# Values of all tokens and keys of the second block by seven products instead of eight

## What is computed

```python
x = x + tanh(g_xattn[0]) * xattn(layernorm(x), ctx, ctx, Wq, Wk, Wv, Wd)
x = x + tanh(g_ffn[0])   * ffn(layernorm(x), gate, up, down)
# xattn: Q = q @ Wq.T  (32 heads of 128)
#        K = k @ Wk.T, V = v @ Wv.T  (8 heads of 128)
#        softmax(causal(Q K^T / sqrt(128))) V, then @ Wd.T; sequences of 64 tokens
# ffn:   w_eff = w * (su @ sv) for gate, up and down; silu(gate) * up, then down
```

## Time and profile before

| | |
|---|---|
| median of three runs | 1504.87 us (1504.06 to 1505.11) |
| the profiled execution | 1504.84 us, its span 1503.0 us |
| PE busy | 1486.7 us, 99% of the span, 7,586 matmuls |
| DVE / POOL / ACT busy | 1081.2 (72%) / 730.1 (49%) / 603.6 us (40%) |
| keys and values | until 193.8 us |
| queries (32 quads) | from 193.8 to about 523 us |
| granted PE clock | 2.4 GHz level, mean 0.999 |
| DMA | 214.4 MB, mean 143 GB/s |

### The profile page before, as it was taken

One profiled execution on the slowest core, in us unless ns is written; L12 is line 12 of the kernel. 1 busy time (PEld: TensorE's weight loads), 2 busy tenths in 40 slices (PEclk: granted clock), 3 DMA queues, 4 the chain that ended last, 5 costly groups with the idle time before them and its releaser, 6 DMA issues.

```text
span 1503.0 us, 21016 instructions
## 1 busy us (share of the span) xinstructions
PE 1486.7 (99%) x7586; PEld 1197.8 (80%) x7586; DVE 1081.2 (72%) x1630; ACT 603.6 (40%) x1040; POOL 730.1 (49%) x636
## 2 busy tenths in 40 slices
PE   8999999999999999999999999999999999999998
PEld 7898978778888777777777777777788888888886
...
GB/s 182 184 195 223 180 195 267 250 239 259 351 304 258 196 184 112 115 132 113 123 145 118 119 127 113 113 153 82 21 44 57 49 56 50 113 50 56 50 57 70
DMA packets 114806, 214.37 MB, mean 143 GB/s; under 512 B 9616, under 2 KB 47760, under 8 KB 112656
## 3 DMA queue, kind: packets, MB, share of 16 engines
...
...
## 4 chain that ended last, share of the span: by engine, by line
PE 91%; DVE 5%; issue 1%; DMA 1%; POOL 1%; ACT 0%; SPq 0%; DVEq 0%; ACTq 0%; POOLq 0%
PE bank L450 67%; PE bank L612 4%; PE bank L574 4%; PE bank L726 3%; PE bank L725 3%; PE bank L727 3%; PE bank L583 2%; PE bank L597 2%; DVE x_st L1057 1%; PE bank L508 1%; DVE er L1078 1%; DMA c_raw<-in_ctx_t 1%; DVE el L1078 1%; DVE X L1243 1%; PE bank L636 0%
## 5 line engine op out<-in xcount | busy, mean ns | idle before, releaser
L1389 POOL TENSOR_TENSOR wd_lo<-wd_raw,wd_hi 128x512 fp32r<-128x512 f32 x64 | 91.4, 1448 | 368.7 <-ACT wd_hi L844 368.7
L450 PE MATMUL bank<-wd_hi,o_hi 128*128 128x512 f32 x512 | 205.7, 402 | 0.0
L450 PE MATMUL bank<-wd_hi,o_lo 128*128 128x512 f32 x512 | 200.1, 391 | 0.0
L450 PE MATMUL bank<-wd_lo,o_hi 128*128 128x512 f32 x512 | 199.3, 389 | 0.0
L450 PE MATMUL bank<-xc_hi,wa_hi 128*128 128x512 f32 x448 | 176.3, 393 | 1.1 <-DVE q_st L1122 0.7
L450 PE MATMUL bank<-xc_lo,wa_hi 128*128 128x512 f32 x448 | 174.7, 390 | 0.0
L450 PE MATMUL bank<-xc_hi,wa_lo 128*128 128x512 f32 x448 | 174.6, 390 | 0.0
L1243 DVE SCALAR_TENSOR_TENSOR X<-bank,tg,X 128x512 f32<-128x512 f32 x224 | 156.4, 741 | 0.0
L450 PE MATMUL bank<-x_hi,wf_hi 128*128 128x512 f32 x392 | 153.0, 390 | 0.2 <-DVE d_lo L1231 0.2
L450 PE MATMUL bank<-x_hi,wf_lo 128*128 128x512 f32 x392 | 152.5, 389 | 0.0
L450 PE MATMUL bank<-x_lo,wf_hi 128*128 128x512 f32 x364 | 141.6, 389 | 0.0
...
## 6 DMA issues: line engine op xcount, KB each, us to landing
...
```

The lines of the kernel that those rows point to most:

```text
L450: last = pe.matmul(to, a, b, start=(start and n == 0), stop=(stop and n == 3 * len(pairs) - 1), skip_group_check=onto)
L1389: g.tensor_tensor(wd_lo[h % 2][:, e, :], wd_raw[:, e, :], f32(wd_hi[h % 2][:, e, :]), ALU.subtract).then_inc(g_wd, 1)
```

## The change

Keys of the first four chunks stay as they were (`keys(0)` to `keys(3)`). All values and the keys of the last four chunks become quads: 8 value quads (quad q makes the values of chunk q; the left-hand side is the chunk's seven combinations, the right-hand side seven combinations of Wv), then 4 key quads (two heads each, over the four chunks together, with combinations of Wk made as for Wq), then the 32 query quads. So there are 44 quads, numbered 0 to 43.

What this adds or moves besides:

- Seven combinations of Wv: four DVE sums (`wv_sums`) and seven ACT and DVE splits of 1,024 elements, among the keys of chunks 1 and 2.
- Seven combinations of each context chunk: four POOL sums of 256 (`c_sums`), three ACT copies (`c_combinations`) and three POOL splits (`c_combinations_lo`, in pieces of 512, 256 and 1,024), for chunk q+2 in quad q. Chunks 1, 2 and 3 are loaded a second time.
- All eight blocks of x are normalised in quads, statistics in quads 0, 3, 5, 7, 10, 13, 16, 19, moments and scaling one quad later, transposes two later and both splits three later. The transposes move from the end of the quad to a place behind product 5.
- The 42 effective weights all lie in quads 0 to 43, none in quads 7 and 8.
- The values of a quad leave in one store from one buffer (`v_st`), which the next quad waits for (`d_vo`).
- Buffers get new places; hi and lo of the combinations of x lie in one tensor `xc`.

The core of the diff:

```diff
 NHP = HKV * G // 2
-NQ = NB * NHP
+NV, NK = NCH, HKV // 2
+Q0 = NV + NK
+NQ = Q0 + NB * NHP
+NW = NQ - NV
...
-    xc_hi = [at(23, "xc_hi0", [P, 7, 2, BT], F32R), at(79, "xc_hi1", [P, 7, 2, BT], F32R)]
-    xc_lo = [at(51, "xc_lo0", [P, 7, 2, BT], F32R), at(107, "xc_lo1", [P, 7, 2, BT], F32R)]
...
+    xc = [at(23, "xc0", [P, 4, 2, 7, 2, P], F32R), at(79, "xc1", [P, 4, 2, 7, 2, P], F32R)]
...
+    c_first = at(47, "c_first", [P, KC, C])
+    c_raw = [at(163, "c_raw0", [P, KC, C]), at(167, "c_raw1", [P, KC, C])]
+    ct = at(171, "ct", [P, 4, 2, P])
...
+    cc = at(79, "cc", [P, 4, 2, 7, 2, P], F32R)
...
+    wk_raw = at(177, "wk_raw", [P, HKV, 512])
+    wvs = at(177, "wvs", [P, 4, 2, 512])
+    wv_hi = at(51, "wv_hi", [P, 7, 2, 512], F32R)
+    wv_lo = at(135, "wv_lo", [P, 7, 2, 512], F32R)
...
+    v_st = at(177, "v_st", [P, HKV, CT, DK])
+    kq = [at(177, "kq0", [P, 2, 4, C]), at(185, "kq1", [P, 2, 4, C])]
...
-    E_KV = NP - NQ
-    E_FROM = NCH - E_KV // 2
-    STATS = {3 * n: 4 + n for n in range(4)}
-    APPLY = {3 * n + 1: 4 + n for n in range(4)}
-    TURN = {3 * n + 2: 4 + n for n in range(4)}
-    COLUMNS = {3 * n + 3: 4 + n for n in range(4)}
-    X_HI = {3 * n + 4: 4 + n for n in range(4)}
-    X_LO = {3 * n + 5: 4 + n for n in range(4)}
-    WD_FIRST = range(24, 28)
...
+    LOADS = [0, 1, 2, 3, *range(1, NCH)]
+    E_GAP = (NV - 1, NV)
+    E_AT = {q: m for m, q in enumerate(q for q in range(NQ) if q not in E_GAP)}
+    E_MOVE = E_AT[NV + 1]
+    STATS = {q: m for m, q in enumerate((0, 3, 5, 7, 10, 13, 16, 19))}
+    APPLY, COLUMNS, X_SPLIT = ({q + n: m for q, m in STATS.items()} for n in range(1, 4))
+    WD_FIRST = range(NQ - 8, NQ - 4)
...
+        def load_c(i):
+            if 3 <= i < 6:
+                sp.wait_ge(a_chi, i - 1)
+                sp.wait_ge(c_split, i - 2)
+            if i >= 6:
+                sp.wait_ge(g_cl, 3 * (i - 4))
+            sp.dma_start(c_buffer(i)[:, :, :], ctx_t[LOADS[i]]).then_inc(d_c[i % 2], 16)
...
+            if q < NV:
+                sp.dma_start(vd[:, q].rearrange("h p t d -> p h (t d)"),
+                             v_st[:, :, :, :].rearrange("p h t d -> p h (t d)")).then_inc(d_vo, 16)
+                return
...
+            w = q - NV
+            m = E_AT[q] if q in E_AT else 0
             if q:
                 store_q(q - 1)
+            if m:
                 store_e(m - 1)
                 load_e(m)
+            if q + 6 < len(LOADS):
+                load_c(q + 6)
+            if q in (NV - 4, NV - 3):
+                load_w(q - NV + 4)
+            if w == 0:
+                load_w(2)
+            if 0 <= w and w + 3 < NW:
+                load_w(w + 3)
...
-        keys(0)
-        keys(1)
-        values(0)
-        values(1)
-        for c in range(2, NCH):
+        for c in range(NCH // 2):
             keys(c)
...
         def product(q, n, to, a, b, onto=False):
-            blk, p = q // NHP, q % 2
-            three_pass(bank[to][:, :],
-                       [((wa_hi[p][:, a, k, :], wa_lo[p][:, a, k, :]),
-                         (xc_hi[blk][:, b, k, :], xc_lo[blk][:, b, k, :])) for k in range(2)],
-                       start=not onto, onto=onto).then_inc(p_p[n], 1)
+            w, s = q - NV, q % 4
+            if q < NV:
+                pairs = [((cc[:, s, 0, b, k, :], cc[:, s, 1, b, k, :]), (wv_hi[:, a, k, :], wv_lo[:, a, k, :]))
+                         for k in range(2)]
+                out = bank[to][:, :]
+            else:
+                right = cc if q < Q0 else xc[block_of(q)]
+                pairs = [((wa_hi[w % 2][:, a, k, :], wa_lo[w % 2][:, a, k, :]),
+                          (right[:, :, 0, b, k, :], right[:, :, 1, b, k, :])) for k in range(2)]
+                out = bank[to][:, :].rearrange("p (s t) -> p s t", s=4)
+            three_pass(out, pairs, start=not onto, onto=onto).then_inc(p_p[n], 1)
         def quad(q):
-            pe.wait_ge(a_wa, 3 * (q + 1))
-            pe.wait_ge(g_wa, 3 * (q + 1))
-            pe.wait_ge(a_xhi, 4 * (q // NHP + 1))
-            pe.wait_ge(v_xlo, 4 * (q // NHP + 1))
-            if q:
+            if q == 0:
+                pe.wait_ge(v_wvl, 7)
+                pe.wait_ge(a_k, 4 * NCH // 2 - 1)
...
             product(q, 5, 2, 3, 3)
+            if q in COLUMNS:
+                columns(COLUMNS[q])
...
-            effective(E_KV + q)
+            if q in E_AT:
+                effective(E_AT[q])
...
-            if q in TURN:
-                columns(TURN[q])
...
+                if 1 <= c <= 2 and 4 * (c - 1) + n < 7:
+                    wv_hi_of(4 * (c - 1) + n)
+        def c_combinations(j):
+            s, raw = j % 4, c_buffer(c_load(j))
+            if j == 0:
+                a.wait_ge(d_c0, 16)
+                a.wait_ge(d_c1, 16)
+            else:
+                a.wait_ge(d_c[c_load(j) % 2], 16 * ((c_load(j) + 1) // 2))
+            a.wait_ge(g_ct, 4 * (j + 1))
+            if 1 <= j <= 3:
+                a.wait_ge(p_k, 4 * NCH // 2)
+                if j == 3:
+                    for n in range(4):
+                        a.wait_ge(d_ko[n], 16 * NCH // 2)
+            if j >= 4:
+                a.wait_ge(p_p[3], j - 3)
+            a.activation(cc[:, s, 0, 0:2, :, :].rearrange("p n k t -> p (n k) t"), raw[:, :, :P],
+                         ACT.Copy).then_inc(a_ch, 1)
+            a.activation(cc[:, s, 0, 2, :, :], raw[:, 2:, P:], ACT.Copy).then_inc(a_ch, 1)
+            a.activation(cc[:, s, 0, 3:7, :, :], ct[:, :, :, :], ACT.Copy).then_inc(a_ch, 1)
...
             a.activation(s5[:, :], bank[2][:, :], ACT.Copy).then_inc(a_s5, 1)
-            if q == 0:
-                left_hi(1)
+            if q + 2 < NCH:
+                c_combinations(q + 2)
...
         keys_out(0)
-        keys_out(1)
         chi(2)
+        c_combinations(0)
         a.wait_ge(d_g, 32)
         a.activation(tg[:, :], graw[:, :], ACT.Tanh).then_inc(a_tanh, 1)
-        for c in range(2, NCH):
-            if c + 1 < NCH:
-                chi(c + 1)
-            keys_out(c)
-            if c >= E_FROM:
-                lr_hi(2 * (c - E_FROM) + 1)
-            if 3 <= c <= 6:
-                x_columns(c - 3)
-                x_hi(c - 3)
-        left_hi(0)
+        keys_out(1)
+        chi(3)
+        keys_out(2)
+        keys_out(3)
+        c_combinations(1)
...
+        def wv_sums():
+            for part in range(5, 9):
+                v.wait_ge(d_w1[part], 16)
+            v.wait_ge(a_w1, HKV)
+            v.wait_ge(v_wk, HKV)
+            a11, a12, a21, a22 = (wv_raw[:, 2 * n:2 * n + 2, :] for n in range(4))
+            v.tensor_tensor(wvs[:, 0], a21, a22, ALU.add).then_inc(v_ws, 1)
+            v.tensor_tensor(wvs[:, 2], a11, a21, ALU.subtract).then_inc(v_ws, 1)
+            v.wait_ge(v_ws, 1)
+            v.tensor_tensor(wvs[:, 1], wvs[:, 0], a11, ALU.subtract).then_inc(v_ws, 1)
+            v.wait_ge(v_ws, 3)
+            v.tensor_tensor(wvs[:, 3], a12, wvs[:, 1], ALU.subtract).then_inc(v_ws, 1)
+        def wv_lo_of(n):
+            k = WV_ORDER[n]
+            raw = wv_raw[:, {0: 0, 1: 2, 2: 6}[k]:{0: 2, 1: 4, 2: 8}[k], :] if k < 3 else wvs[:, k - 3, :, :]
+            v.wait_ge(a_wvh, n + 1)
+            v.wait_ge(v_ws, 4)
+            v.tensor_tensor(wv_lo[:, k, :, :], raw, f32(wv_hi[:, k, :, :]), ALU.subtract).then_inc(v_wvl, 1)
...
+            if 1 <= q <= NV:
+                v.wait_ge(d_vo, 16 * q)
...
+            if q in E_AT and q < NQ - 2:
+                effective(E_AT[q])
+            if q in X_SPLIT:
+                x_lo(X_SPLIT[q])
...
+        def c_sums(j):
+            raw = c_buffer(c_load(j))
+            if j == 0:
+                g.wait_ge(d_c0, 16)
+                g.wait_ge(d_c1, 16)
+            else:
+                g.wait_ge(d_c[c_load(j) % 2], 16 * ((c_load(j) + 1) // 2))
+                g.wait_ge(a_ch, 3 * j)
+                g.wait_ge(g_cl, 3 * j)
+            b11, b12, b21, b22 = raw[:, :2, :P], raw[:, :2, P:], raw[:, 2:, :P], raw[:, 2:, P:]
+            g.tensor_tensor(ct[:, 0], b12, b11, ALU.subtract).then_inc(g_ct, 1)
+            g.tensor_tensor(ct[:, 2], b22, b12, ALU.subtract).then_inc(g_ct, 1)
+            g.wait_ge(g_ct, 4 * j + 1)
+            g.tensor_tensor(ct[:, 1], b22, ct[:, 0], ALU.subtract).then_inc(g_ct, 1)
+            g.wait_ge(g_ct, 4 * j + 3)
+            g.tensor_tensor(ct[:, 3], ct[:, 1], b21, ALU.subtract).then_inc(g_ct, 1)
+        def c_combinations_lo(j):
+            to, raw = cc[:, j % 4], c_buffer(c_load(j))
+            g.wait_ge(a_ch, 3 * j + 1)
+            g.tensor_tensor(to[:, 1, 0:2].rearrange("p n k t -> p (n k) t"), raw[:, :, :P],
+                            f32(to[:, 0, 0:2]).rearrange("p n k t -> p (n k) t"), ALU.subtract).then_inc(g_cl, 1)
+            g.wait_ge(a_ch, 3 * j + 2)
+            g.tensor_tensor(to[:, 1, 2], raw[:, 2:, P:], f32(to[:, 0, 2]), ALU.subtract).then_inc(g_cl, 1)
+            g.wait_ge(a_ch, 3 * j + 3)
```

(28 more changed lines are left out.)

454 lines of the change are left out of this document (211 added, 243 removed).

## The result

The changed kernel takes **1509.56 us** (median of 6 runs, 1507.59 to 1511.62) beside 1505.02 for the kernel before on the same chip: ratio 1.0030, 95% interval 1.0017 to 1.0043. It is slower by 4.5 us; the forecast was 1499.5, and what came is the rival *the turn waits for DVE*, at 27.8 us of stalls and not the 35.4 of its long bounds. The profiled execution is the fastest of the six, 1507.59 us with a span of 1505.6 (before: 1503.0).

A forecast was written before the change was run, and what follows sets the result against it. PE's matmuls and its stops were taken to bound the kernel: 1504.84 - 18.8 (work shed) - 6.3 (old stalls) + 19.8 (new stalls at quad 0 and the blocks of x) = 1499.5 us, range 1488 to 1512.

The forecast's parts named there:

- the turn waits for DVE: Rival, chance 0.25: scaling late, PE stands mid-quad; 35.4 us of stalls at its long bounds, 1515 us; decides from 25.1.
- What PE sheds: On PE, keys of four chunks and all values go (133.3 us), twelve quads come (114.5): -18.8 us.
- Old stalls: Quads 0 to 15 of the kernel before: normalising x within quads cost 6.3 us of PE stalls, which go: -6.3 us.
- covered work at nothing: Added ACT and DVE work among the first keys, and reloads of three chunks, hide behind other work: 0 us.
- Quad 0: End of quad 0: ACT's copy freeing bank 0 waits behind POOL's sums of chunk 2, delaying quad 1: +2.2 us.
- Block 1: First block of x in the quads: scaling waits for POOL's power behind the low parts of chunk 3: 1.0 us.
- block 2: Second block of x: low part and statistics at one quad's end, POOL behind: 3.4 us.
- Blocks 5 to 8: Each loses 0.3 us at DVE's split of factors, 0.55 at product 5, 1.5 at the turn: 4 x 2.35 = 9.4 us.
- Blocks 3 and 4: Blocks of x two quads apart, low part and scaling at one quad's end: 1.5 and 1.7 us.
- The rule on the shared SBUF interfaces: POOL contends with DVE instructions having two SBUF inputs or a 2-port mode; 12 more quads of POOL work run beside DVE.
- DVE takes it: Rival, chance 0.20: blocks of x cost what they did or less, the turn waits for nothing: 1491.5 us.
- One value buffer: Rival: value quads wait for the store; at 8.4 us landing each of eight loses 0.8: 1506 us; chance 0.13 including slower products.

The follow-up runs named there:

- run with the pieces: Two runs: changed kernel with POOL's 1,024-element low part in four pieces, in every quad with it (1495.80 us) or only in quads that turn x (1499.30 us).

## Why the prediction was wrong

*What PE sheds, -18.8 us*: right. Quad 0 began at 54.4 us (54.6 forecast), quads 3 and 6 took 9.77 us, quad 8, without an effective weight, 9.52, and 13 late quads 127.0: the reading of the right-hand sides in four pieces costs nothing.

*Old stalls, -6.3, and covered work at nothing*: right as a sum (1507.5 against 1507.59 with the stalls measured); no product of the keys waits for ACT.

*Quad 0, +2.2*: 2.05, and for the cause named. *Block 1, 1.0 and block 2, 3.4*: 0.8 and 3.2, but block 2's not where I had put them: the turn of quad 5 waits for nothing, and the stops lie at the effective weight of quad 4 and at products in quads 4 and 5.

*Blocks 5 to 8, 4 x 2.35 = 9.4*: 14.7, and this is the step that failed: the length of the scaling, by which the turn's wait was priced. The timing of DVE held to its last instruction but one: from the start of quad q with statistics I had moments ending at 20.5, the last quarter at 23.1 and the scaling starting at 23.7; the rows above, from 168.0, give 20.5, 23.0 and 23.6. `el` and `er` cost 0.41 us (0.3 forecast) and product 5 0.44 (0.55). Then I let the scaling take 2.7 us and the turn lose 1.5. It took 3.61, and since the second four transposes wait for its end, the turn lost 0.9 more: 2.4 us, 3.6 for the four blocks. I had 3.08 us for the two halves at hand and took 2.7 without a reason; that is 0.4 of the 0.9. The other 0.5 is the order: in that row the first half got ahead of POOL's long piece (0.54, then 2.62), in the changed kernel it did not, and the second half then met one more POOL instruction (2.74, then 0.95). I did not look at the two halves apart, nor at when POOL's piece began.

*Blocks 3 and 4, 1.5 and 1.7*, for which I showed no working: 2.4 and 4.2. Of these 3.4 us too much 1.6 are a slow stretch. The other 1.8 come by another way than in blocks 5 to 8, since the scaling took only 1.81 us in quad 7 and 2.34 in quad 9. In quad 9 it started 0.60 us late for POOL's power, and the rows of DVE and of POOL say why:

```profile
155.01 2.18 DVE L1152 TENSOR_TENSOR xc<-xb,xc 128x1792 fp32r<-128x1792 f32 x1
157.78 2.34 DVE L1146 TENSOR_SCALAR x_st<-x_st,mean,rstd 128x512 f32<-128x512 f32 x2 [0.60 <-POOL rstd L1431]
```

```profile
155.26 2.48 POOL L1431 TENSOR_TENSOR rstd<-veps,neg_half 128x2 f32<-128x2 f32 x1
```

The power takes 0.70 us in quad 12 and 2.48 here: it ended 0.6 us behind DVE's low part of x, which was running when it came up. POOL waits for DVE as DVE waits for POOL. It fits that neither run with the pieces took away quad 9's wait; no run tests it by itself. In quad 7 the scaling stands behind a low part of 3.12 us, which I had at 2.7.

The rest, some 3 us (the 1.6 of quad 9 and as much in quad 15), is the clock, which stood in no case: two stretches of the lower level behind turn waits of 1.59 and 1.98 us in the profiled run, and more in the others, which puts the median 2 us above the profiled run. The kernel before had shorter waits and 0.999. These parts make 8.6 us; quad 0, blocks 1 and 2 and the rest came in 0.6 below the forecast.

*The rule on the shared SBUF interfaces* (the Trainium skill, GPSIMD Engine Reference, Key points) was the right one to weigh. How long one engine waits stands in the Trainium skill, SBUF — State Buffer, under Who interferes with whom: whichever of the two engines issues first has the shared ports for the whole instruction, and the other blocks; `tensor_scalar` is among the VectorE operations that can take part. These runs agree, in both directions: the scaling's first half ended 0.3 us behind POOL's piece, and in the kernel before, where that half got ahead, POOL's piece took 2.67 us at 280.98 and not the 2.36 of the changed kernel. So the order of the two engines decides which instruction waits, and that is what my term lacked.

*Rivals.* *The turn waits for DVE* was described with its place and engine, with 25.1 us of stalls as the point from which it decides; 27.8 came. I gave it 0.25 because DVE's sum fitted; its last term decided. *DVE takes it* held for the turns of quads 2 and 5, which wait for no scaling, and fell at that of quad 7. *One value buffer*: stores of values landed in 4.7 us (5.5 at most), and no value quad waits for one. The range, 1488 to 1512, held the time.
